# Scores of three small attention layers from their own rows, and one projection with a premade query-key product

## What is computed

```python
# layer 0
q = Wq @ xf + bq;  k = Wk @ xf + bk;  v = Wv @ xf + bv        # q, k have 32 rows
x = x + v @ softmax(q.T @ k).T
# layer 1
f = Wf @ xf + bf;  g = Wg @ xf + bg;  h = Wh @ xf + bh        # f, g have 8 rows
x = gamma * (h @ softmax(f.T @ g).T) + x
# layer 2
q = Wq @ xt;  k = Wk @ xt;  v = Wv @ xt                       # 64 rows each
x = gamma * (v @ softmax(q.T @ k).T) + x
# layer 3: group norm, 8 heads of 8 rows, output projection, global feature, residual
```

## Time and profile before

| | |
|---|---|
| median of 3 runs | 101.08 us (101.0 to 101.27) |
| span of the profiled execution | 100.9 us |
| PE matmul busy | 87.6 us (87%) |
| DVE busy | 66.3 us (66%) |
| ACT busy | 47.3 us (47%) |
| POOL busy | 22.5 us (22%) |
| chain that ended last, by engine | PE 66%, DVE 20%, ACT 9%, issue 3% |
| granted TensorE clock, mean | 0.914 |

### The profile page before, as it was taken

The page is one execution under the profiler, slowest core; times in us unless marked ns, Lnnn a source line. Parts: engine busy times, 40 slices in busy tenths (PEclk is TensorE's granted clock), DMA queues, the critical chain, the costliest instruction groups (busy, mean ns, idle before and its releaser), DMA issues.

```text
span 100.9 us, 1683 instructions
## 1 busy us (share of the span) xinstructions
PE 87.6 (87%) x577; PEld 65.2 (65%) x577; DVE 66.3 (66%) x178; ACT 47.3 (47%) x111; POOL 22.5 (22%) x46
## 2 busy tenths in 40 slices
PE   5996977699899999766994999999999899999660
PEld 5874735478679687464893899766776675566220
DVE  1247699978674997598566627788968875543401
ACT  3329366445595525300232242727665848766310
POOL 7963000000000020212075276087043000000000
PEclk9999999999999999996559655999999999999975
DMA  2940000000000000000000000000000000000101
GB/s 69 307 186 0 0 0 0 6 0 0 0 3 3 0 0 0 0 0 6 0 0 0 0 0 0 0 0 6 0 0 0 0 6 0 0 3 0 52 6 52
DMA packets 1304, 1.79 MB, mean 18 GB/s; under 512 B 144, under 2 KB 912, under 8 KB 1296
## 3 DMA queue, kind: packets, MB, share of 16 engines
q1 hardware_dynamic: 1008, 1.48, 4.5%
q10 hardware_dynamic: 288, 0.20, 0.7%
HBM read 1.42 MB, written 0.26 MB: 17 GB/s over the span
## 4 chain that ended last, share of the span: by engine, by line
PE 66%; DVE 20%; ACT 9%; issue 3%; DVEq 0%
PE PS L446 11%; PE PS L479 9%; PE PS L466 7%; PE PS L432 6%; PE PS L294 6%; PE PS L341 6%; ACT E L709 6%; DVE KM L983 3%; PE PS L456 3%; DVE NM L989 3%; PE PS L353 3%; DVE NM L878 3%; PE PS L490 2%; DVE E L894 2%; PE PS L304 2%
## 5 line engine op out<-in xcount | busy, mean ns | idle before, releaser
L989 DVE TENSOR_REDUCE NM<-PS 128x2 f32<-128x512 f32 x32 | 21.9, 690 | 7.0 <-PE PS L446 6.8
L742 ACT ACTIVATE E<-PS 128x1024 f32<-128x1024 f32 x16 | 16.3, 1024 | 11.6 <-PE PS L466 11.6
L269 POOL TENSOR_TENSOR KM<-QKS,W 128x512 fp32r<-128x512 f32 x14 | 14.3, 1041 | 21.0 <-ACT QKS L733 21.0
L446 PE MATMUL PS<-KM,QKS 128*128 128x256 f32 x64 | 15.6, 335 | 3.8 <-DVE KM L983 2.5
L709 ACT ACTIVATE E<-PS,NM 128x256 f32<-128x256 f32 x24 | 11.1, 473 | 11.9 <-DVE NM L878 11.8
L446 PEld LDWEIGHTS PS<-KM,QKS 128*128 128x128 f32 x64 | 11.1, 218 | 7.4 <-DVE NM L989 3.6
L294 PE MATMUL PS<-idle 128*128 128x256 f32 x65 | 13.7, 350 | 1.2 <-DVE idle L838 1.2
L294 PEld LDWEIGHTS PS<-idle 128*128 128x128 f32 x65 | 11.0, 233 | 3.1 <-DVE idle L838 1.2
L466 PE MATMUL PS<-QSA,KM 128*128 128x256 f32 x64 | 11.5, 305 | 0.0
L466 PEld LDWEIGHTS PS<-QSA,KM 128*128 128x128 f32 x64 | 9.5, 207 | 0.8 <-issue 0.8
L479 PE MATMUL PS<-E,VA 128*32 128x256 f32 x128 | 9.8, 390 | 0.0
(11 more groups left out here) (104 smaller groups left out, 131.0 us busy)
## 6 DMA issues: line engine op xcount, KB each, us to landing
W<-pack SPq DMA_DIRECT2D x1, 384.0 KB, 5.4
W<-pack SPq DMA_DIRECT2D x1, 290.0 KB, 4.9
X<-x SPq DMA_DIRECT2D x2, 128.0 KB, 2.6
W<-pack SPq DMA_DIRECT2D x1, 256.0 KB, 4.5
out<-Y SPq DMA_DIRECT2D x2, 128.0 KB, 1.7
W<-pack ACTq DMA_DIRECT2D x1, 128.0 KB, 3.0
W<-pack ACTq DMA_DIRECT2D x1, 72.0 KB, 2.5
```

What stands on the lines that cost most here:

```text
L269: pool.tensor_tensor(KM[p][s % 3][:, heads, :], QKS[p][s % 3][:, 1:2, :].bitcast(f32).broadcast_to([P, 2, N]), w("heads")[:, heads].unsque ...
L446: mm = pe.matmul(bank_a[p][:, half * N:(half + 1) * N], QKS[p][s % 3][:, 0, half * HALF:(half + 1) * HALF], KM[p][s % 3][:, j, :], start=T ...
L742: act.activation(E3[p][s % 2][m][:, :, :].rearrange("k j q -> k (j q)"), bank_bc[p][:, :], ACT.Exp, scale=float(HD) ** -0.5)\
L989: dve.tensor_reduce(NM3[p][:, s % 2, :, j], bank_a[p].rearrange("q (h k) -> q h k", h=2), AX.X, ALU.max, negate=True).then_inc(maxima3[p], 1)
```

## The change

Layers 0 to 2 make the scores of both images in one call. For each half of the queries, image 0's matmul (rows 0 to 31, or 0 to 63 in layer 2) is followed by image 1's (rows 32 to 63, or 64 to 127), each with its own 32 or 64 rows of queries and keys, in banks a and b. No padded keys are left, so the zeroing on POOL goes, ACT's copies of image 1's keys go, and DVE copies both images' keys of layer 0 at once. In layer 2 the scores are made as (A2 x)^T x with A2 the product of the query and key weights: it is made once, early, by a matmul (`query_key_product`) behind the scores of layer 0's pair 1 and a copy on ACT (`product_out`) between two exponents. Layer 2 then projects once for each pair, its keys are `X[p]` itself, and the copies of keys of layer 2 are gone on both engines.

```diff
@@ scores, projection
+                if layer == 2 and p == 0:
+                    pe.wait_ge(a2_out, 1)
+                lhs = A2[:, :] if layer == 2 else w(f"w{layer}")
+                pe.matmul(bank_a[p][:, 0:N], lhs, X[p][:, :], start=True, stop=True)\
+                    .then_inc(q_made[p], 1)
+
+            def query_key_product():
+                pe.wait_ge(w_loaded[2], 16)
+                pe.matmul(bank_d[1][:, N:N + P], w("nq2"), w("nk2"), start=True, stop=True)\
+                    .then_inc(a2_made, 1)
+
+            def score(layer, p):
+                pe.wait_ge(q_out[p], layer + 1)
                 if layer < 2:
-                    pe.matmul(bank_a[p][:, 0:N], w(f"w{layer}"), X[p][:, :], start=True, stop=True)\
-                        .then_inc(q_made[p], 1)
-                    return
-                pe.matmul(bank_a[p][:, 0:N], w(f"wq{layer}"), X[p][:, :], start=True, stop=True)\
-                    .then_inc(q_made[p], 1)
-                pe.matmul(bank_b[p][:, 0:N], w(f"wk{layer}"), X[p][:, :], start=True, stop=True)\
-                    .then_inc(k_made[p], 1)
...
+                    pe.wait_ge(k_out[p], layer + 1)
+                lhs = (Qs, F1, Qs)[layer][p]
+                rhs = (K0s, G1, X)[layer][p]
+                size = C if layer == 2 else QUAD
                 for half in range(2):
-                    mm = pe.matmul(bank[:, half * N:(half + 1) * N], halves(lhs, rows, half),
-                                   rhs, start=True, stop=True)
-                mm.then_inc(scores[p], 1)
+                    for b in range(2):
+                        rows = slice(b * size, (b + 1) * size)
+                        bank = (bank_a, bank_b)[b][p]
+                        mm = pe.matmul(bank[:, half * N:(half + 1) * N], halves(lhs, rows, half),
+                                       rhs[rows, :], start=True, stop=True)
+                        if half == 1:
+                            mm.then_inc(scores[p], 1)
@@ ACT
-                    act.wait_ge(prep_pool, p + 1)
-                    rows = slice(3 * HID0, 4 * HID0)
-                    act.activation(K0s[p][HID0:2 * HID0, 1, :], bank_a[p][rows, 0:N], ACT.Identity,
-                                   bias=col("b0")[rows, :]).then_inc(k_out1[p], 1)
...
+            def product_out():
+                act.wait_ge(a2_made, 1)
+                act.activation(A2[:, :], bank_d[1][:, N:N + P], ACT.Copy).then_inc(a2_out, 1)
...
             exponents(0, 0, 1)
+            product_out()
             exponents(0, 1, 1)
@@ DVE
-            keys(2, 0)
...
-            keys(2, 1)
```

More of the change, by code:

```diff
@@ L54 @@
     [("ident", P), ("w1", P), ("wv1", P), ("vb1", P)],
-    [("wq2", P), ("wk2", P), ("wv2", P), ("fold", C), ("gavg", P), ("heads", HPG)],
+    [("nq2", P), ("nk2", P), ("wv2", P), ("fold", C), ("gavg", P), ("heads", HPG)],
     [("wq3", P), ("wk3", P), ("wv3", P), ("vb3", P), ("wg3", P), ("wp3", P)],
@@ L133, in conv_attention_chain @@
         Qs = pair_sb("Q", [P, N])
-        K0s = pair_sb("K0", [2 * HID0, 2, N])
-        Ks = pair_sb("K", [P, 2, N])
+        K0s = pair_sb("K0", [2 * HID0, N])
+        A2 = sb("A2", [P, P])
         V = pair_sb("V", [P, 2, P])
@@ L184, in conv_attention_chain @@
         q_out, k_out, v_out = pair_sem("q_out"), pair_sem("k_out"), pair_sem("v_out")
-        k_out1 = pair_sem("k_out1")
+        a2_made = ctx.enter_context(nc.semaphore("a2_made"))
+        a2_out = ctx.enter_context(nc.semaphore("a2_out"))
         high_out = pair_sem("high_out")
@@ L225, in _ @@
                 sp.wait_ge(stored[p], 16)
-        ZEROED = 5 * PAIRS + len(sel) + 1
+        ZEROED = 3 * PAIRS + len(sel) + 1
         PREPARED = ZEROED + 2 * PAIRS + 1 + 2 * KINDS3
@@ L232, in _ @@
         def _(pool):
[L233 to L236, removed]
             for p in R:
@@ L327, in score @@
[L327 to L339, removed]
-                for half in range(2):
-                    mm = pe.matmul(bank[:, half * N:(half + 1) * N], halves(lhs, rows, half),
-                                   rhs, start=True, stop=True)
-                mm.then_inc(scores[p], 1)
+                if layer == 2 and p == 0:
+                    pe.wait_ge(a2_out, 1)
@@ L513, in _ @@
             values(0, X[0], 0)
-            score(0, 0, 0)
-            score(0, 1, 0)
+            score(0, 0)
             keep_clock(2, 0)
@@ L520, in _ @@
             values(0, X[1], 1)
-            score(0, 0, 1)
             turn(0, 1, 0)
-            score(0, 1, 1)
+            score(0, 1)
+            query_key_product()
             mix(0, 0)
@@ L529, in _ @@
             turn(0, 1, 1)
-            score(1, 0, 0)
-            score(1, 1, 0)
+            score(1, 0)
             mix(0, 1)
@@ L537, in _ @@
             mix(1, 0)
-            score(1, 0, 1)
-            score(1, 1, 1)
+            score(1, 1)
             keep_clock(6, 0)
@@ L543, in _ @@
             values(2, X[0], 0)
-            score(2, 0, 0)
-            score(2, 1, 0)
+            score(2, 0)
             mix(1, 1)
@@ L551, in _ @@
             values(2, X[1], 1)
-            score(2, 0, 1)
             turn(2, 1, 0)
-            score(2, 1, 1)
+            score(2, 1)
             mix(2, 0)
@@ L687, in queries @@
                                    bias=col("b0")[rows, :]).then_inc(q_out[p], 1)
-                    act.wait_ge(prep_pool, p + 1)
-                    rows = slice(3 * HID0, 4 * HID0)
-                    act.activation(K0s[p][HID0:2 * HID0, 1, :], bank_a[p][rows, 0:N], ACT.Identity,
-                                   bias=col("b0")[rows, :]).then_inc(k_out1[p], 1)
                 else:
-                    rows = slice(C, P)
                     act.activation(Qs[p][:, :], bank_a[p][:, 0:N], ACT.Copy).then_inc(q_out[p], 1)
[L695 to L698, removed]
+            def product_out():
+                act.wait_ge(a2_made, 1)
+                act.activation(A2[:, :], bank_d[1][:, N:N + P], ACT.Copy).then_inc(a2_out, 1)
             def values2(p):
@@ L719, in high_parts @@
             def high_parts(p):
-                act.wait_ge(k_made[p], 2)
+                act.wait_ge(k_made[p], 1)
                 act.wait_ge(stat[p], 9)
@@ L854, in keys @@
                     return
[L855 to L865, removed]
+                rows = slice(2 * HID0, 4 * HID0)
+                dve.wait_ge(q_made[p], 1)
+                dve.tensor_scalar(K0s[p][:, :], bank_a[p][rows, 0:N], col("b0")[rows, :], None,
+                                  ALU.add).then_inc(k_out[p], 1)
             def add_value_bias(layer, p):
@@ L1197, in packed @@
     both("wv1", i["L1_conv_Wh"].T)
-    both("wq2", i["L2_conv_Wq"].T)
-    both("wk2", i["L2_conv_Wk"].T)
+    both("nq2", i["L2_conv_Wq"])
+    both("nk2", i["L2_conv_Wk"])
     both("wv2", i["L2_conv_Wv"].T)
```

## The result

The changed kernel took 104.1 us in the median of four runs (103.32 to 104.72) against 101.17 us (101.0 to 105.33) for the kernel before beside it: a ratio of 1.0296, with a 95% interval from 1.0206 to 1.0386. I had forecast 99.45 us, in a range from 96.6 to 101.2. In all, the kernel before ran 42 times: 97.92 to 109.03 us, median 101.7. The changed one ran 10 times: 99.5 to 105.38, median 103.5. By these longer lists it is 1.8 us slower and not 2.9.

A forecast was written before the change was run, and what follows sets the result against it. The prediction took one long dependent chain to bound the kernel, with PE on it most. From 101.08 us it took 1.08 (layer 2) and 0.55 (last projection) to reach 99.45 us, range 96.6 to 101.2.

The forecast's parts named there:

- Row tiles overlap in float32: Scores of layers 0 and 2: four float32 row-tile matmuls run beside each other, in about 1.1 us and not 1.96.
- pair 1's first exponent 0.30 us earlier: Layer 0: ACT begins pair 1's exponents at 13.31 and not 13.61.
- The copy of the product: Layer 0: new ACT step amid pair 1's four exponents, some 0.28 us, leaving layer 0 a gain of 0.02 us.
- Layer 1: nothing: Layer 1: tiles already overlap and VectorE and ACT bind it, so gain 0.
- Layer 2: I had 1.08 us: Layer 2: pair 0's residual starts at 33.53 against 34.61, 1.08 us earlier.
- pair 1's layer-1 exponents now start 0.40 earlier: Start of layer 2 on ACT: without the key copy, pair 1's layer-1 exponents start 0.40 us earlier.
- So my sum keeps 1.08: Layer 3: an earlier clock fall costs about 1.4 us, an earlier return gives it back, so the 1.08 us shift stays.
- A spell as long as the other two, 6.8 us, then ends near 49.4: Layer 3: half-speed spell starts near 42.6, keeps its 6.8 us length and ends near 49.4, not 52.8.
- rival 2: Layer 3: clock falls at about 42.6, full speed returns only at 52.8; end at 101.4 us; chance 12%.
- rival 3: Layer 0: thinner PE work loses the clock, adding some 1.5 us between 9 and 15 us; end at 101.5; chance 5%.
- the base: Whole kernel: 101.08 us median and 100.9 us profiled span lie 0.2 us apart, so trace shifts come off the median.
- the tail: End of layer 3: pair 1's last projection finishes before the clock falls, 0.54 us and not 1.13; 0.55 counted.

The follow-up runs named there:

- e4: Changed kernel with the product's matmul ahead of pair 0's first turn in layer 0 and its copy ahead of pair 1's exponents; median 100.5 us.
- e7: Changed kernel with keep-clock matmuls in PE's four longest gaps (10 in layer 0; 9, 5 and 11 in layer 3); 97.37 us.
- e11: Layer 0's part alone, on the kernel before, with keep-clock matmuls in PE's four longest gaps, 10 in layer 0; 98.06 us.
- e5: The changed kernel run again, unchanged, for the spread; 99.5 to 105.38 us, median 103.07.
- e2: Layer 0's part alone (row tiles and new order, no product, layer 2 as before), against the kernel before; median 102.3 us.
- e1: Layer 2's part alone (layer 0's padded scores, key copies and order back), against the kernel before; median 100.31 us, ratio 0.987.
- e3: Changed kernel with ten more keep-clock matmuls ahead of pair 0's first turn in layer 0; 101.15 us.
- e9: Changed kernel with keep-clock matmuls in layer 3's gaps only (9, 5 and 11), none added in layer 0; 97.6 us.
- e6: Kernel before with keep-clock matmuls in PE's four longest gaps (6 in layer 0; 9, 5 and 11 in layer 3); 98.59 us.
- e10: Layer 2's part alone, on the kernel before, with keep-clock matmuls in PE's four longest gaps, 6 in layer 0; 99.0 us.
- e12: e7 with the scores issued image by image, not alternately; 96.95 us, 0.957 of the kernel before.

## Why the prediction was wrong

**Right in kind, too small in size: the edits.** Row tiles overlap in float32: 1.13 us for the four matmuls, as assumed, for 1.96.

Layer 0: I had pair 1's first exponent 0.30 us earlier, of which I counted 0.15 ahead of the first maximum. That part came (e4's profile). Behind the maximum that leaves 0.15 of my forecast, and it is 0.27: the exponent comes 6.49 us later in e7 (7.01 to 13.50) and 6.76 before (6.85 to 13.61); e11, up to the residual, has 0.25. The copy of the product took 0.28 us as I had it, but it put only 0.15 to 0.17 on the chain: from the first of the four exponents to the end of the last it is 2.10 us in e7 (13.50 to 15.60) and 1.93 before (13.61 to 15.54). Layer 1: nothing, as said.

Layer 2: I had 1.08 us, it is 1.25. The step that was too small is "pair 1's layer-1 exponents now start 0.40 earlier". Measured from pair 0's residual of layer 1 it is 2.85 us in the kernel before and 2.29 in e7, so 0.56. First the kernel before (the earlier trace rows has its queries at 24.84 and its keys at 25.25), then e7:

```profile
22.80 0.47 DVE L909 SCALAR_TENSOR_TENSOR X<-PS,W,X 128x256 f32<-128x256 f32 x1
...
25.65 0.47 ACT L709 ACTIVATE E<-PS,NM 128x256 f32<-128x256 f32 x1
```

```profile
22.87 0.47 DVE L896 SCALAR_TENSOR_TENSOR X<-PS,W,X 128x256 f32<-128x256 f32 x1
...
24.90 0.38 ACT L687 ACTIVATE Q<-PS 128x256 f32<-128x256 f32 x1
...
25.16 0.48 ACT L702 ACTIVATE E<-PS,NM 128x256 f32<-128x256 f32 x1
```

Before, the keys started 0.41 behind the queries and the exponent 0.40 behind the keys; in e7 the exponent starts 0.26 behind the queries, ahead of their end. From pair 1's scores to the residual it is 2.37 us in e7 (31.05 to 33.42) where I had 2.38. In sum the edits at full clock are worth 1.33 us behind the first maximum and some 0.15 ahead of it, where I forecast 1.08.

**Wrong, the clock.** The step that failed is "So my sum keeps 1.08". It took the clock of one profiled execution for a property of the kernel, let it fall some 3 us earlier and return as much earlier ("A spell as long as the other two, 6.8 us, then ends near 49.4"). In the changed kernel's profile it fell at 44.5, stayed down until 54.7, over 10 us, and PE's small jobs lay in it just as rival 2 had them. Measured from pair 0's residual of layer 2, the fall was well placed: I had it 9.1 us behind, and it came at 9.3, 9.0 (e5) and 9.4 (e4). The return was not: I had it 15.9 us behind, and in these three profiles it came at 19.2 to 19.7. In the kernel before and in e2 the clock fell 11.4 us behind the residual and returned at 18.2, in e1 and e3 it fell at 13.7 and 14.0 and returned at 17.1 and 17.4. So in the seven profiles without fillers in layer 3 an earlier fall meant a longer spell (3.4, 6.8 or 10.2 us), not a spell of the same length moved. And it fell in layer 0 as well: rival 3, to which I gave 5%, with a price of 1.5 us where 0.95 (e9) to 1.1 was measured. I saw that the scores would stream 0.9 us less per pair, and gave it little weight. e3, e7 and e9 show that the loss is the clock's: fill PE's gaps, and the lost time comes back. They do not show which part of the change brings it (see below).

**Wrong, the base.** "The 101.08 us median and the 100.9 us span of the profiled execution are 0.2 us apart, so a shift worked out in the trace is taken off the median as it stands." The timed runs with both numbers show that this kernel's time is its span plus 2.2 us (101.0 us has a span of 98.8 or so). The profiled execution of 100.9 us was thus one of about 103.1 us, worse in its clock (0.914) than the three timed ones (which ran at times that go with 0.96). I took a gain off a median that had never had some of the losses I read in the trace, among them part of the half-speed time. Taken off 103.1, the same sum gives 101.5.

**Wrong, the tail** (0.55 us for the last projection at full speed). In the changed kernel's profile the clock fell at 99.1 just as the projection began at 99.05 (1.15 us). In its second profile (e5), with nothing changed, the clock held until behind it, and the projection took 0.68 us:

```profile
98.24 0.68 PE PS L504 x2
```

So this gain is not the edit's. Over the fourteen profiles the projection took 0.68 or 0.69 us in seven and 0.97 to 1.21 in the others, whichever kernel it was. And at full clock it is worth 1.13 - 0.68 = 0.45 and not 0.55; pair 0's 0.54 was no measure of it.

**Open.** Which part of the change lowers the clock is not settled. Each part alone leaves the mean clock where the kernel before has it (medians 0.953 and 0.953, before 0.950), both together bring it to 0.898, and moving the product's matmul alone (e4), with PE's work unchanged, brings it back to 0.946. So "PE has less to do" does not explain it by itself; where the work stands seems to matter too, and no run parts the two. Nor is it settled why the early spell in layer 0 goes together with a long one in layer 3 (both profiles of the changed kernel have the two, e4's has the long one alone, e2's has the early one with a spell of 6.8 us). Also open: the changed kernel and all its relatives have 1.7 to 2.0 us outside the span, the kernel before and e6 2.1 to 2.3. That gain of some 0.35 us, not in my sum, came with each of e1 and e2, which share no edit but two memsets less on GpSimd; I did not try that alone.

## What to carry to other kernels

Before a cut on PE, look at how often the clock changes from run to run, with the list of mean clocks and not with one profile: a kernel whose executions lie at 0.90, 0.93, 0.96 and 0.98 has its losses there, and a cut that saves 1.3 us of chain can, as here, lose more than that by the clock. First put matmuls on zeros into PE's gaps until the clock stays up (here 31 of them were worth 3 us to the kernel before, and 35 of them 6 us to the changed one), then cut; the cut then shows its own worth, here 1.3 us of chain. Do not move a spell along with the kernel at its old length: here its length changed with where it began. Add what lies outside the span before a profile is set beside a median.

## What the runs showed of the hardware

The same program, unchanged, took 97.9 to 109.0 us, and the time followed the granted clock in the main (97.9 us at 0.990, 101 at 0.962, 103.3 at 0.913, 105.4 at 0.898), but not always: the 109.0 us had 0.951. The first rise came between 4.6 and 14.5 us after the start, with the same nine keep-clock matmuls issued from 1.2 us on in each. The record of the clock reads 1.00 ahead of its first change although the matmuls run at half pace there, so a mean clock near 1 can hide a bad start (e10: 98.8 us of span at 0.988).

In the changed kernel's profile the granted clock fell to 1.2 GHz at 10.4 us, in layer 0, after 3 us in which PE had 1.19 us of busy time; the longest gap in them was 1.8 us, ahead of pair 0's turn. In the kernel before it fell at 46.0 us, and the longest gap of PE in the 4 us before that was 1.1 us.

Two float32 matmuls in different row tiles of 32 or of 64 rows run fully beside each other (1.13 us for four of 256 columns, with the switch of tiling in it), whichever is issued first (1.14 us in e12). The switch itself costs PE 0.20 us by the earlier trace rows: 0.10 in the start (0.54 against 0.44) and 0.10 in the length (1.13 against 1.03). The Trainium skill (TensorEngine Tiling (Array Packing), Key Properties) has it that a change of tiling mode drains the engine. The rows agree that a switch costs; no run here shows that a drain is what costs.
